# Key and value projections of a cross attention as three float16 products instead of one float32 product, with a scale for each batch

## The reference, cut to what matters

```python
def _mha_cross(x, mem, in_w, in_b, out_w, out_b):
    q = _split_heads(x @ wq.T + bq, H)
    k = _split_heads(mem @ wk.T + bk, H)     # mem: (32, 1601, 128)
    v = _split_heads(mem @ wv.T + bv, H)
    scores = jnp.einsum('bhqd,bhkd->bhqk', q, k) * (1.0 / math.sqrt(hd))
    attn = jax.nn.softmax(scores, axis=-1)
    out = _merge_heads(jnp.einsum('bhqk,bhkd->bhqd', attn, v))
    return out @ out_w.T + out_b
```

## Time and profile before

| what | value |
|---|---|
| median of 3 runs | 3556.06 us (3551.76 to 3568.44) |
| the profiled execution's own time | 3552.84 us |
| span of its trace | 3551.1 us |
| mean granted TensorE clock | 0.964 of full speed |
| busy: TensorE, weight loads | 3326.5 us, 2375.5 us |
| busy: VectorE, ScalarE, GpSimd | 2495.5 us, 1909.4 us, 1102.6 us |

### The profile page before, as it was taken

The page is one execution under the profiler, slowest core; times in us unless marked ns, Lnnn a source line. Parts: engine busy times, 40 slices in busy tenths (PEclk is TensorE's granted clock), DMA queues, the critical chain, the costliest instruction groups (busy, mean ns, idle before and its releaser), DMA issues. The chain is left out here.

```text
span 3551.1 us, 83011 instructions
## 1 busy us (share of the span) xinstructions
PE 3326.5 (94%) x32677; PEld 2375.5 (67%) x32913; DVE 2495.5 (70%) x7178; ACT 1909.4 (54%) x2964; POOL 1102.6 (31%) x795
## 2 busy tenths in 40 slices
PE   7789999999998788999999999999999999797999
PEld 5646666666666666677777777777777777565666
DVE  6757777777775443777777777777777777577544
ACT  4336666666565232566666666666666666344333
POOL 1033333334330001444434433444344333130000
PEclk9979999999999688999999999999999999898999
DMA  1023333333320011111111111111111110100000
GB/s 54 19 64 79 72 76 76 75 82 71 75 65 10 2 48 33 43 32 43 43 33 32 43 34 32 42 43 35 31 42 43 34 31 22 48 1 28 1 1 13
DMA packets 96677, 146.45 MB, mean 41 GB/s; under 512 B 14976, under 2 KB 74400, under 8 KB 95520
## 3 DMA queue, kind: packets, MB, share of 16 engines
q1 hardware_dynamic: 96288, 141.12, 14.8%
HBM read 100.66 MB, written 1.05 MB: 29 GB/s over the span
## 5 line engine op out<-in xcount | busy, mean ns | idle before, releaser
L2263 DVE SCALAR_TENSOR_TENSOR arena<-banks,arena 128x512 f16<-128x512 f32 (+1 forms) x1024 | 554.5, 583 | 308.6 <-ACT arena L2352 307.2
L2352 ACT ACTIVATE arena<-banks 128x512 f16<-128x512 f32 (+1 forms) x1024 | 471.3, 512 | 400.1 <-PE banks L2170 397.1
L1103 DVE TENSOR_REDUCE arena<-banks 128x1 f32<-128x512 f32 (+1 forms) x896 | 529.7, 628 | 187.6 <-PE banks L988 182.4
L1200 ACT ACTIVATE arena<-banks 128x1024 f32<-128x1024 f32 (+1 forms) x448 | 425.1, 964 | 316.5 <-PE banks L1009 313.5
L2275 DVE CUSTOM_DVE_ANT_0 arena<-banks,arena 128x1024 f32<-128x1024 f32 (+1 forms) x512 | 494.4, 987 | 32.1 <-issue 31.9
L2359 ACT ACTIVATE arena<-arena 128x1601 f32<-128x1601 f32 x256 | 417.7, 1632 | 107.8 <-DVE arena L2281 105.8
L2170 PE MATMUL banks<-consts,arena 128*128 128x128 f32 (+1 forms) x3328 | 456.8, 275 | 7.1 <-DVE arena L2263 7.0
L2184 PE MATMUL banks<-arena 128*128 128x256 f16 (+1 forms) x1664 | 456.1, 274 | 0.7 <-ACT arena L2366 0.7
L2186 PE MATMUL banks<-arena 128*128 128x256 f16 (+1 forms) x1664 | 451.3, 271 | 0.0
L2185 PE MATMUL banks<-arena 128*128 128x256 f16 (+1 forms) x1664 | 450.2, 271 | 0.0
L2170 PEld LDWEIGHTS banks<-consts,arena 128*128 128x128 f32 (+1 forms) x3328 | 364.8, 141 | 17.3 <-issue 10.1
(11 more groups left out here) (360 smaller groups left out, 6119.2 us busy)
## 6 DMA issues: line engine op xcount, KB each, us to landing
arena<-in_ctxT SPq DMA_DIRECT2D x64, 800.5 KB, 4.4
arena<-arena SPq DMA_DIRECT2D x768, 50.0 KB, 2.2
arena<-in_ctx SPq DMA_DIRECT2D x32, 768.0 KB
arena<-in_mask SPq DMA_DIRECT2D x32, 200.1 KB, 4.5
arena<-in_m2w SPq DMA_DIRECT2D x3, 2048.0 KB, 8.1
arena<-in_xw SPq DMA_DIRECT2D x1, 2048.0 KB, 11.6
weights<-in_weights SPq DMA_DIRECT2D x1, 1920.0 KB, 12.2
arena<-in_ctx SPq DMA_DIRECT2D x32, 32.5 KB
```

Source lines behind the costliest of these rows:

```text
L1103: eng.tensor_reduce(o, s, AX, ALU.max).then_inc(a_max, 1)
L1200: eng.activation(pr[0:w, at % 4, :].rearrange("p (x n) -> p x n", x=2)[:, :, 0:n], c.ps[0:w, bank:bank + 2, 0:n], ACT.Exp, scale=scale).th ...
L2263: eng.scalar_tensor_tensor(out=part(ptl, g, gr), in0=turned(gr), scalar=TOP, in1=part(pth, g, gr), op0=ALU.mult, op1=ALU.subtract).then_in ...
L2352: eng.activation(part(pth, g, gr), turned(gr), ACT.Copy, scale=TOP).then_inc(t_high, 1)
```

## The change

For all batches but those of the first pair, the context is scaled to the range of float16 and split into two float16 halves, `ch` and `cl`; the two weight matrices are scaled and split once, into `wh` and `wl`. A projection is then ch wh + ch wl + cl wh, three float16 products into the same place in PSUM, and ScalarE multiplies by the product of the two units when it moves the result out.

The scale of a batch comes about so: ScalarE sums the magnitudes of each row of the context (`magnitudes`, into `ch` as a scratch place), GpSimd puts the 128 sums on a diagonal (`diagonal`), TensorE multiplies that by ones, which gives every partition all the sums (`ctx_row`, bank 7), VectorE takes their maximum, a floor, the inverse and the units (`ctx_scale`), and GpSimd scales the context in place and splits it (`split_ctx`: three passes over 1601 columns). `ctx_row` and `ctx_scale` stand in step 6 of a key unit, behind the queries; the first of them in step 4 of the first unit. The context's loads now wait until the split has read the buffer, and are issued at other places. Apart from this, the copy L1110 in `spread_max` becomes a product with ones.

```diff
@@ sp
         def load_ctx(i, b):
-            bb, made = i * 2 + b, i * 8 + 4 * b - 4
-            wait_if(eng, v_ps, made)
+            bb = i * 2 + b
+            if i == 1:
+                eng.wait_ge(v_ps, 4 * b + 4)
+            if i > 1:
+                eng.wait_ge(c_split, batch_no(i - 1, b) + 1)
...
         def body(i, more):
-            if more:
-                load_ctx(i + 1, 0)
+            if i == 0 and more:
+                load_ctx(1, 0)
+            if i > 0 and more:
+                load_ctx(i + 1, 1)
             spread_keys(i, 1, 0)
             spread_keys(i, 1, 1)
+            if i == 0 and more:
+                load_ctx(1, 1)
+            if i + 2 < PAIRS:
+                load_ctx(i + 2, 0)
             if more:
-                load_ctx(i + 1, 1)
                 spread_keys(i + 1, 0, 0)
                 spread_keys(i + 1, 0, 1)
@@ pool
+        def diagonal(i, b):
+            n = batch_no(i, b)
+            eng.wait_ge(c_total, n + 1)
+            wait_if(eng, c_row, n)
+            eng.tensor_tensor(diag_c, c.C("ident"), total[:, b, :].to_broadcast([P, P]), ALU.mult).then_inc(c_diag, 1)
+
+        def split_ctx(i, b):
+            n = batch_no(i, b)
+            x = ctxT[:, b, :]
+            eng.wait_ge(c_inverse, n + 1)
+            eng.tensor_tensor(x, x, per_c[:, b, :].to_broadcast([P, S]), ALU.mult).then_inc(c_scaled, 1)
+            eng.wait_ge(c_scaled, n + 1)
+            if i > 1:
+                eng.wait_ge(v_ps, (i - 1) * 8 + 4 * b + 4)
+            eng.tensor_tensor(ch[:, b, 0:S], x, c.one[:].to_broadcast([P, S]), ALU.mult).then_inc(c_high, 1)
+            eng.wait_ge(c_high, n + 1)
+            eng.tensor_tensor(cl[:, b, 0:S], x, ch[:, b, 0:S], ALU.subtract).then_inc(c_split, 1)
...
             if more:
-                for b in range(2):
-                    split_keys(i + 1, b)
-                    split_queries(i + 1, b)
+                split_keys(i + 1, 0)
+                diagonal(i + 1, 1)
+                split_queries(i + 1, 0)
+                split_ctx(i + 1, 1)
+                split_keys(i + 1, 1)
+                if i + 2 < PAIRS:
+                    diagonal(i + 2, 0)
+                split_queries(i + 1, 1)
+                if i + 2 < PAIRS:
+                    split_ctx(i + 2, 0)
@@ pe
             if n == 0:
-                eng.wait_ge(ctx_loaded[b], i * 16 + 16)
...
+                eng.wait_ge(w_low, 2)
+                eng.wait_ge(c_split, batch_no(i, b) + 1)
+            eng.matmul(o, wh[:, 0, :], ch[:, b, a:z], start=True, stop=False)
+            eng.matmul(o, wh[:, 0, :], cl[:, b, a:z], start=False, stop=False)
+            eng.matmul(o, wl[:, 0, :], ch[:, b, a:z], start=False, stop=True).then_inc(k_ps, 1)
...
+                    eng.matmul(o, ch[:, b, r], wh[:, 1, :], start=True, stop=False)
+                    eng.matmul(o, ch[:, b, r], wl[:, 1, :], start=False, stop=False)
+                    mm = eng.matmul(o, cl[:, b, r], wh[:, 1, :], start=False, stop=True)
...
+        def weights_row():
+            take_bank7((w_top, 1))
+            eng.wait_ge(ones_set, 1)
+            eng.wait_ge(w_diag, 2)
+            eng.matmul(c.ps[:, 7, 0:2 * P], ones, diag_w.rearrange("p w n -> p (w n)"), start=True, stop=True).then_inc(w_row, 1)
+
+        def ctx_row(i, b):
+            n = batch_no(i, b)
+            take_bank7((c_top, n + 1))
+            eng.wait_ge(c_diag, n + 1)
+            eng.matmul(c.ps[:, 7, 2 * P:3 * P], ones, diag_c, start=True, stop=True).then_inc(c_row, 1)
...
+                    if st == 6 and v == 1 and more:
+                        ctx_row(i + 1, 1)
+                    if st == 6 and v == 3 and i + 2 < PAIRS:
+                        ctx_row(i + 2, 0)
@@ dve
-            eng.tensor_copy(mxs[:, :, 0], mx).then_inc(mx_high, 1)
+            eng.tensor_tensor(mxs[:, :, 0], mx, c.one[:].to_broadcast([P, 4]), ALU.mult).then_inc(mx_high, 1)
...
+        def ctx_scale(i, b):
+            n = batch_no(i, b)
+            eng.wait_ge(c_row, n + 1)
+            eng.tensor_reduce(top_c, c.ps[:, 7, 2 * P:3 * P], AX, ALU.max).then_inc(c_top, 1)
+            eng.wait_ge(range_set, 1)
+            eng.wait_ge(c_top, n + 1)
+            eng.scalar_tensor_tensor(out=floor_c, in0=top_c, scalar=1e-25, in1=per_range, op0=ALU.max, op1=ALU.mult).then_inc(c_floor, 1)
+            eng.wait_ge(c_floor, n + 1)
+            eng.reciprocal(per_c[:, b, :], floor_c).then_inc(c_inverse, 1)
+            if i > 1:
+                eng.wait_ge(v_made, (i - 1) * 8 + 4 * b + 4)
+            eng.tensor_tensor(units[:, b, :], per_top, floor_c.to_broadcast([P, 2]), ALU.mult).then_inc(c_units, 1)
...
@@ act
-            eng.activation(kf[:, a:z], c.ps[:, 7, 0:z - a], ACT.Identity, bias=c.W("c_bk")).then_inc(k_copied, 1)
...
+            eng.activation(o, ps, ACT.Identity, bias=c.W("c_bk"), scale=units[:, b, 0:1]).then_inc(k_copied, 1)
...
+                eng.activation(o, s, ACT.Identity, scale=units[0:w, b, 1:2]).then_inc(v_made, 1)
+
+        def magnitudes(i, b):
+
+            eng.wait_ge(ctx_loaded[b], i * 16 + 16)
+            if i > 1:
+                eng.wait_ge(v_ps, (i - 1) * 8 + 4 * b + 4)
+                eng.wait_ge(c_diag, batch_no(i - 1, b) + 1)
+            eng.activation(ch[:, b, 0:S], ctxT[:, b, :], ACT.Abs, accum_out=total[:, b, :]).then_inc(c_total, 1)
...
+                    if st == 5 and v == 0 and more:
+                        magnitudes(i + 1, 1)
+                    if st == 5 and v == 2 and i + 2 < PAIRS:
+                        magnitudes(i + 2, 0)
```

More of the change, by code:

```diff
@@ L819, in cross_attention_0 @@
     om, s1, rd = k.f32(4, L), k.f32(L), k.f32(L)
-    sem = lambda n: c.sem(f"x0_{n}")
+    ch, cl = k.f16(2, S + 1), k.f16(2, S + 1)
+    wh, wl = k.f16(2, D), k.f16(2, D)
+    ones, diag_w, diag_c = k.f32(P), k.f32(2, P), k.f32(P)
+    peak_w, top_w, per_top, to_f16 = (k.f32(2) for _ in range(4))
+    total, top_c, floor_c, per_c = k.f32(2, 1), k.f32(1), k.f32(1), k.f32(2, 1)
+    units, per_range = k.f32(2, 2), k.f32(1)
+    TOP = 32768.0
+    sem = lambda n: c.sem(f"x0_{n}")
+    ones_set, w_peaks, w_diag, w_row, w_top, w_floor, w_inverse, w_high, w_low = (sem(f"w_{n}") for n in (
+        "ones", "peaks", "diag", "row_psum", "top", "floored", "inverse", "high", "low"))
+    c_total, c_diag, c_row, c_top, c_floor, c_inverse, c_units = (sem(f"ctx_{n}") for n in (
+        "total", "diag", "row_psum", "top", "floored", "inverse", "units"))
+    range_set = sem("range_set")
+    c_scaled, c_high, c_split = sem("ctx_scaled"), sem("ctx_high"), sem("ctx_split")
     two = lambda n: [sem(f"{n}{i}") for i in range(2)]
@@ L845, in unit_no, with batch_no @@
         return i * UNITS + v
+    def batch_no(i, b):
+        return (i - 1) * 2 + b
     def pairs(eng, body):
@@ L938, in keys @@
             take_bank7((k_copied, i * 8 + 4 * b + n + 1))
-            if n == 0:
-                eng.wait_ge(ctx_loaded[b], i * 16 + 16)
-            a, z = chunks[n]
-            eng.matmul(c.ps[:, 7, 0:z - a], c.W("c_wk"), ctxT[:, b, a:z], start=True, stop=True).then_inc(k_ps, 1)
+            a, z = chunks[n]
+            o = c.ps[:, 7, 0:z - a]
+            if i == 0:
+                if n == 0:
+                    eng.wait_ge(ctx_loaded[b], 16)
+                eng.matmul(o, c.W("c_wk"), ctxT[:, b, a:z], start=True, stop=True).then_inc(k_ps, 1)
+                return
+            if n == 0:
+                eng.wait_ge(w_low, 2)
[3 more added lines that the diff above has]
+            eng.matmul(o, wl[:, 0, :], ch[:, b, a:z], start=False, stop=True).then_inc(k_ps, 1)
         def values(i, b, n):
@@ L1071, in body @@
                             final(*later(i, v, -1))
+                        elif more:
+                            ctx_row(1, 0)
                     elif st == 6 and v % 2 == 1 and more:
@@ L1169, in body @@
                         final(*later(i, v, -1))
+                    if st == 4 and not old and more:
+                        ctx_scale(1, 0)
                     if st == 5 and here(1):
@@ L1183, in keys @@
             wait_if(eng, k_split, i * 8 + 4 * b + n - 3)
-            eng.activation(kf[:, a:z], c.ps[:, 7, 0:z - a], ACT.Identity, bias=c.W("c_bk")).then_inc(k_copied, 1)
+            o, ps = kf[:, a:z], c.ps[:, 7, 0:z - a]
+            if i == 0:
+                eng.activation(o, ps, ACT.Identity, bias=c.W("c_bk")).then_inc(k_copied, 1)
+                return
+            if n == 0:
+                eng.wait_ge(c_units, batch_no(i, b) + 1)
+            eng.activation(o, ps, ACT.Identity, bias=c.W("c_bk"), scale=units[:, b, 0:1]).then_inc(k_copied, 1)
         def values(i, b, n):
@@ L1214, in body @@
                     exps(i, v, st)
+                    if i + v == 0 and st == 0 and more:
+                        magnitudes(1, 0)
+                    if st == 5 and v == 0 and more:
+                        magnitudes(i + 1, 1)
+                    if st == 5 and v == 2 and i + 2 < PAIRS:
+                        magnitudes(i + 2, 0)
```

42 lines of the change are left out of this document (39 added, 3 removed).

## The result

The changed kernel takes 3660.86 us (median of 4 runs, 3653.39 to 3666.64) against 3554.9 for the kernel before on the same chip: **slower by 2.9%**, ratio 1.0289 with a 95% interval of 1.0256 to 1.0322. The forecast was 3550 in a range of 3525 to 3580.

What follows compares the result with a forecast made beforehand. TensorE was taken to bound a unit's first slots, VectorE its tail. Thirty repeats saving 0.67 us each gave 20 us saved against 14 lost at the start: 6 less, so 3550 us, range 3525 to 3580.

Steps and rivals of the forecast that it cites:

- the maxima's high half: In VectorE's spreading of the maxima: a product of two tensors escapes GpSimd's hold, gaining 0.16 us per key unit.
- VectorE is held by GpSimd: Maxima spreading in value units waits about 2.3 us for GpSimd's third pass, program about 3620 us; chance 0.08.
- products of microseconds on VectorE: Trace sign against the forecast: VectorE's products taking microseconds, where spreading products were expected at 0.17 during GpSimd's passes.
- Key chunks: Key projections on TensorE: three float16 products plus exposed weight load take 0.75 us, where float32 took 1.05.
- value chunks: Value projections on TensorE: twelve float16 products of 128 columns plus exposed load take 0.77 us, where float32 took 1.09.
- The halves are in time: GpSimd's split halves are ready 12.4 us after the query bias; TensorE wants them about 14.7 after, slack 2.3.
- No further table loads: Trace sign on ScalarE: its sums of magnitudes need no other function table, so their cost stays covered.
- The start: Before the steady repeats: weight scaling, ScalarE's first pass, the first scaled batch and clock recovery lose 14 us, between 9 and 20.
- the wait for the first halves: At the start, TensorE stands still 6.5 us before the first float16 keys; the trace sign says 6.
- The sum of a repeat: A key unit plus a value unit: 0.74 + 0.16 - 0.23 = 0.67 us saved of 27.88.
- the value of the maxima's exchange: Replacing the copy by a product of two tensors in the maxima's spreading gains 0.16 us per key unit.
- The chain's price where it stands: Scale chain behind the query bias costs 1.16 us, making a value unit 0.23 longer; chain bounds 0.9 and 1.5.

Runs made afterwards that it cites:

- the passes in pieces: The changed kernel with each of GpSimd's three passes cut into four instructions of at most 512 columns: 3696.55 us.
- the chain with one tensor each: The changed kernel with the scale chain's floor and units written with scalar operands on one column, three instructions for two: 3669.43 us.
- the timed version: The changed kernel with GpSimd's third pass and third key chunk's low half waiting for VectorE's maxima spreading, and scalar operands in the scale chain: 3552.29 us, ratio 0.9996.

## Why the prediction was wrong

**The step that failed** is the one under the maxima's high half: "So a product of two tensors is not held, the copy is." It rested on the product at 637.36 in the earlier trace rows, of which the prediction says that it ran wholly inside a GpSimd instruction in 0.23, its usual time. That is a misreading: the instruction ended at 637.50 and the product at 637.59, 0.09 later. What the copy at 636.80 had met is GpSimd's instruction before, a row that the prediction does not show:

```profile
636.79 0.30 POOL L897 TENSOR_TENSOR arena<-arena,one 128x65 bf16<-128x65 f32 x1
```

The copy ended at 637.13, 0.04 after it. So a hold is read from the two ends, and by the ends the product at 637.36 cannot decide the question. It began 0.14 before the GpSimd instruction's end, so without a hold it ends 0.09 after it. With the passes in pieces the same product is held in 29 value units, where it takes 1.07 to 1.14, and ends 0.08 after the piece. The two readings differ by 0.01. That products are held like the copy is shown by 634.74 in the kernel before, by 652.99 in the changed one, and by the copy's equal 1.98 in its place. One row carried two terms of the sum (the 0.16 saved, and the 0.17 for each small instruction of the chain) and dismissed a rival.

**The rival "VectorE is held by GpSimd" was right in mechanism** and had 0.08; "products of microseconds on VectorE" was also named as a sign of being wrong. In the repeats of all runs, instructions of VectorE with two inputs in SBUF were held when they met a GpSimd instruction, and so was the copy of four columns; reductions and the query bias (one input in PSUM) were not. The Trainium skill's rule (SBUF — State Buffer, section "SBUF: two separate sides"), cited in the prediction as against the row, says this, and of copies in a two-port mode as well: whichever of the two engines starts first has the shared ports until its instruction ends. The runs agree with it (1.98 and 2.85); whether the copy is in such a mode, no row shows.

The rival's place was right too, the third pass of a value unit. Its price was too low. It said 2.3 a repeat over the forecast, to 3620; measured are 3.75 (30.96 less 27.21), to 3661. The shortest repeat without a stretch at half clock, 30.16, is 2.95 over the forecast, and the rows account for it: 1.56 at the high half of the value unit (1.73 for 0.17), 0.61 at that of the key unit (0.78), 0.25 at the floor and 0.53 at the units. The holds in the chain and in the value unit are not independent, as the chain with one tensor each showed: what the first does not take, the second does. In most other repeats the key unit's high half is near its usual time (0.24), and TensorE's clock makes up for more than that: the two repeats with a granted clock of 1.00 take 30.16 and 30.17, most have 0.94 or 0.95 and take 30.7 to 31.3, and the four with 0.89 take 31.9 to 32.4. I priced a wait as its own length and left out what TensorE's clock does after it.

**Right, step by step.** Key chunks are 0.75 on TensorE at full clock and value chunks 0.77, as forecast. A key chunk after:

```profile
665.86 0.39 PE L1004 MATMUL banks<-arena 128*128 128x512 f16 x1
...
666.61 0.51 PE L1110 MATMUL banks<-arena 128*32 128x192 f32 x5
```

For value chunks the page's 81 ns for a load and product of 128 columns (the Trainium skill, TensorE: Matmul & The Clock Gate, section "Back-to-back issue gap") would have given 0.97 by the prediction's estimate, and the trace does not agree with it. VectorE idles 0.58 between query bias and reduction (0.5), the reduction takes 0.29 (0.30), the passes 2.85, 2.86 and 3.0 to 3.26 (2.85, 2.85, 3.0). The halves are in time, 12.3 to 12.5 after the query bias's end (12.4): no steady repeat has TensorE waiting for them, and the third pass even bears a further wait of 1.5. No further table loads. **The start** was forecast at 14. The query bias that opens the first repeat comes 12.4 later, of which 6.5 had passed before the stage's first projection, and the first repeat is 8.1 longer: 14.0. The 6.5 are no effect of the change: the first projection comes anywhere from 175.1 to 183.4 in the executions with the changed code. Behind the total, the wait for the first halves was smaller than forecast, 3.27 for 6, and TensorE also waited 1.67 for an exponent behind ScalarE's second sum of magnitudes; that the clock cost about 2 had no row of its own in the prediction, and no run isolates it.

**The sum of a repeat** was 27.21; with the holds timed away it is 27.30, and the program 3552 instead of the forecast 3550. So the sum over VectorE's and TensorE's rows held within 0.1, and the miss of 111 us comes from one interaction between two engines that the sum had taken as independent, with the clock behind it. One term is off for certain, the value of the maxima's exchange, 0.03 for 0.16; in the timed version the same 0.15 is gained by GpSimd being elsewhere. The chain's price where it stands (1.16) is not contradicted; moving it recovered 0.38 where I had expected 0.85, and which of the two places costs more than I reckoned stays open. Part of the sum's agreement may be two errors that cancel; no run excludes it.

## What to carry to other kernels

Before giving GpSimd long instructions, list every VectorE instruction with two inputs in SBUF, or with one input there and more than one column (reductions apart), however small, and see what of GpSimd it would meet; compare the ends of the two, not the duration with its usual value. A small instruction in a dependent chain costs as much as what it meets, and cutting the long one into pieces can make it worse. One wait on the engine with slack (here GpSimd, 1.5 us later) can undo the collision, as long as nothing makes that engine late: a faster loop ran into its DMAs, and a second buffer paid more than a further wait. If an edit that removes time upstream changes nothing, look for the wait that grew by the same amount: it names the engine that sets the length.

## What the runs showed of the hardware

- Held instructions of VectorE of up to four columns end 0.01 to 0.04 us after the GpSimd instruction they met: 1.98, 2.85, 2.62 or 0.30 us for one of 128x4 that takes 0.17 or 0.18 alone. A product of 64 columns, 0.23 alone, ends 0.08 after it (1.14).
- A reduction of 16 columns of one SBUF tensor was not held within the same GpSimd pass (0.17), nor were instructions with scalar operands on one column beside the splitting of the queries (0.15 to 0.20); the copy of four columns from float32 to bfloat16 was, although it has one input too.
- One tensor is not enough to escape. At the start of the stage, in the changed kernel, instructions with one tensor and scalars on 2 and 128 columns are held, VectorE's rows first:

```profile
216.31 0.73 DVE L1239 TENSOR_SCALAR arena<-arena 128x2 f32<-128x2 f32 x1
...
217.28 1.05 DVE L1245 TENSOR_SCALAR arena<-weights,arena 128x128 f16<-128x128 f32 x1
```

```profile
215.98 1.04 POOL L923 TENSOR_TENSOR arena<-arena,one 128x512 bf16<-128x512 f32 x1
217.09 1.15 POOL L925 TENSOR_TENSOR arena<-arena 128x512 bf16<-128x512 f32 x1
```

They end 0.02 and 0.09 after the GpSimd instruction. The one of two columns takes 0.17 at this place in two later versions, where it hardly meets GpSimd. So only the form with one column is shown to be free.
- GpSimd is held by VectorE as well. Its product of 128x512, 1.04 alone, took 4.15 at 186.34, beside VectorE's copy of 128x6408 (3.48), and ended 0.89 after the copy.
- The third pass takes 3.02 for one batch of a pair and 3.25 for the other, in turn, in the changed kernel and in the versions in which VectorE's chain no longer meets it. So that chain does not make the difference; what does was not tried.
- In the repeat shown, after 1.72 us of idling, TensorE ran at 1.2 instead of 2.4 GHz (0.61 for a product that takes 0.40 at 663.97), and the program with such gaps in most repeats has a mean clock of 0.947 instead of 0.964.
